# A four-layer block on one core: the order of y, z and the clamp on VectorE and ScalarE, and the place of one product on TensorE

## The reference, cut to what matters

```
proj = h @ in_proj_w.T                        # gate, x, B, C and dt
hBC  = silu(conv4(x, B, C))                   # causal, 4 taps, one filter per channel
dt   = softplus(dt + dt_bias);  A_dt = -exp(A_log) * dt;  x_dt = x * dt
# chunks of 128 tokens, two in a sequence; 128 heads of 64, in 8 groups that share B and C
Y_diag = (C·B * exp(segment_sum(A_dt))) @ x_dt            # within a chunk
Y_off  = C @ (state left by the chunk before) * decay     # across, second chunk of a sequence only
y = Y_diag + Y_off + D * x
y = rmsnorm(y) * norm_w * silu(gate)
out = y @ out_proj_w.T
```

## Time and profile before

| | us |
|---|---|
| median of 3 runs | 1646.56 |
| the profiled execution | 1649.56 |
| its span, first to last instruction | 1647.8 |
| PE busy in the span | 1592.1 (97%) |
| PE weight loads busy | 1305.5 (79%) |
| DVE busy | 1358.0 (82%) |
| ACT busy | 1281.6 (78%) |
| POOL busy | 801.7 (49%) |

### The profile page before, as it was taken

The page is one execution under the profiler, slowest core; times in us unless marked ns, Lnnn a source line. Parts: engine busy times, 40 slices in busy tenths (PEclk is TensorE's granted clock), DMA queues, the critical chain, the costliest instruction groups (busy, mean ns, idle before and its releaser), DMA issues.

```text
span 1647.8 us, 27075 instructions
## 1 busy us (share of the span) xinstructions
PE 1592.1 (97%) x8984; PEld 1305.5 (79%) x8984; DVE 1358.0 (82%) x2199; ACT 1281.6 (78%) x2218; POOL 801.7 (49%) x806
## 2 busy tenths in 40 slices
PE   6999999999999999999999999999999999999988
PEld 5888777788888887888788788888788888888766
DVE  5887886888888888887888887898888888878766
ACT  4454459888989798979987898888888888798842
POOL 3565124554556455545554454544554555454460
PEclk9999999999999999999999999999999999999999
DMA  5320345455565446545555455545554645445321
GB/s 174 120 91 1 111 133 155 143 161 148 140 179 153 146 130 176 155 129 150 170 143 160 135 170 143 173 115 172 152 160 131 166 145 160 144 142 161 116 71 52
DMA packets 186074, 229.56 MB, mean 139 GB/s; under 512 B 22384, under 2 KB 122096, under 8 KB 184272
## 3 DMA queue, kind: packets, MB, share of 16 engines
q1 hardware_dynamic: 185936, 227.84, 46.6%
HBM read 190.02 MB, written 37.75 MB: 138 GB/s over the span
## 4 chain that ended last, share of the span: by engine, by line
PE 43%; DVE 20%; issue 9%; ACT 7%; DMA 7%; SPq 1%; POOL 1%; DVEq 0%; ACTq 0%; POOLq 0%
PE bank L160 8%; PE bank L162 7%; PE bank L161 7%; DVE m_xc L1955 7%; PE bank L2343 4%; PE bank L2347 4%; PE bank L2309 4%; PE bank L2344 4%; DMA m_x_rows<-x_turned_rows 4%; DMA x_turned_rows<-m_x_blocks 3%; DVE m_gate L1955 3%; ACT m_mt L1661 2%; DVE m_y L2047 2%; PE bank L2331 2%; DVE xdt L2000 1%
## 5 line engine op out<-in xcount | busy, mean ns | idle before, releaser
L160 PE MATMUL bank<-xh,w_h 128*128 128x512 f32 x1152 | 463.4, 402 | 6.9 <-DVE m_xc L1955 3.9
L162 PE MATMUL bank<-xh,w_l 128*128 128x512 f32 x1152 | 450.9, 391 | 0.0
L161 PE MATMUL bank<-xl,w_h 128*128 128x512 f32 x1152 | 450.5, 391 | 0.0
L1569 POOL TENSOR_TENSOR m_z_l<-m_zg,m_z_h 128x512 fp32r<-128x512 f32 x128 | 179.4, 1401 | 458.2 <-ACT m_z_h L1715 458.2
L1551 POOL TENSOR_TENSOR w_l<-w_raw,w_h 128x512 fp32r<-128x512 f32 x142 | 203.6, 1434 | 228.2 <-ACT w_h L1629 228.2
L1661 ACT ACTIVATE m_mt<-m_mt,m_unit 128x128 f32<-128x128 f32 x1024 | 312.3, 390 | 0.0
L160 PEld LDWEIGHTS bank<-xh,w_h 128*128 128x128 f32 x1152 | 217.1, 188 | 61.9 <-issue 18.9
L162 PEld LDWEIGHTS bank<-xh,w_l 128*128 128x128 f32 x1152 | 216.9, 188 | 46.1
L1955 DVE SCALAR_TENSOR_TENSOR m_xc<-bank,m_par_slots,m_xc 128x1020 f32<-128x1020 f32 (+2 forms) x192 | 243.9, 1270 | 9.9 <-ACT m_xc L1640 5.4
L161 PEld LDWEIGHTS bank<-xl,w_h 128*128 128x128 f32 x1152 | 217.4, 189 | 40.4
L2343 PE MATMUL bank<-m_wo_h,m_z_h 128*128 128x512 f32 x512 | 205.0, 400 | 9.2 <-ACT m_z_h L1715 8.6
(11 more groups left out here) (315 smaller groups left out, 2857.2 us busy)
## 6 DMA issues: line engine op xcount, KB each, us to landing
m_mt<-ncs_rows SPq DMA_DIRECT2D x128, 512.0 KB, 5.8
w_raw<-w_in SPq DMA_DIRECT2D x144, 256.0 KB, 4.2
x_turned_rows<-m_x_blocks SPq DMA_DIRECT2D x120, 256.0 KB, 3.9
m_x_rows<-x_turned_rows SPq DMA_DIRECT2D x480, 64.0 KB, 2.3
m_wo_raw<-w_out_in SPq DMA_DIRECT2D x64, 256.0 KB, 3.9
m_e<-ecs_rows SPq DMA_DIRECT2D x128, 128.0 KB, 3.7
a_wo_raw<-wo_in SPq DMA_DIRECT2D x8, 1024.0 KB, 5.0
x<-x_in SPq DMA_DIRECT2D x8, 256.0 KB, 4.3
```

The source lines that it names most:

```text
L160: nc.tensor.matmul(out, ah, bh, start=first, stop=False)
L161: nc.tensor.matmul(out, ah, bl, start=False, stop=False)
L162: return nc.tensor.matmul(out, al, bh, start=False, stop=last)
L1569: nc.gpsimd.tensor_tensor(z_l[:, s % 2, :, :], zg[:], f(z_h[:, s % 2, :, :]), ALU.subtract).then_inc(zl_ready, 1)
```

## The change

Four edits go together. Nothing is added or taken away; every engine runs the same operations on the same tiles, in another order.

1. VectorE, paired steps: y and z of chunk s-1 are made ahead of `add_out(s-2)` and, in even steps, ahead of `times_dt(s)`. In odd steps they stay behind the first block transpose.
2. ScalarE: `decay` is cut into `clamp` (the eight Relu) and `decay` (the exponential). Outside steps 1 and 9 the order is clamp, z's high part, square, exponential; it was clamp, exponential, square, high part. In steps 1 and 9 only high part and square change places.
3. TensorE: `across` stands right behind the pair's masked products in every odd step; it stood between the two halves of the step's tile.
4. GpSimd: where the last group's second half begins and in it, `to_chunk_end` of chunk s+1 is made at the end of odd step s, not at the end of step s+1.

```
@@ gpsimd, step @@
-                if s % 2 == 0 and own(kind):
+                if s % 2 == 0 and own(kind) and paired(kind, s):
                     to_chunk_end(g, s)
+                if s % 2 == 1 and turned_by_tensor(kind, s):
+                    to_chunk_end(g, s + 1)
@@ scalar @@
-            def decay(g, s):
+            def clamp(g, s):
...
                 last.then_inc(clamped, 1)
+
+            def decay(g, s):
+                g, s = g + s // STEPS, s % STEPS
                 act.wait_ge(clamped, at(g, s))
...
             def square_and_high(g, s):
+                act.wait_ge(z_ready, at(g, s))
+                act.wait_ge(out_done, at(g, s - 2))
+                nc.scalar.activation(z_h[:, s % 2, :, :], zg[:], ACT.Copy).then_inc(zh_ready, 1)
                 act.wait_ge(y_ready, at(g, s))
                 act.wait_ge(sq_summed, at(g, s - 1))
                 nc.scalar.activation(ysq[:], y[:], ACT.Square).then_inc(sq_ready, 1)
-                act.wait_ge(z_ready, at(g, s))
-                act.wait_ge(out_done, at(g, s - 2))
-                nc.scalar.activation(z_h[:, s % 2, :, :], zg[:], ACT.Copy).then_inc(zh_ready, 1)
@@ scalar, step @@
-                if ahead(kind, s + 2) and not (kind == "lead" and s == STEPS - 1):
+                clamps = ahead(kind, s + 2) and not (kind == "lead" and s == STEPS - 1)
+                if clamps:
+                    clamp(g, s + 2)
+                if clamps and not (paired(kind, s) and t != 1):
                     decay(g, s + 2)
...
                 if paired(kind, s) and t != 1:
                     for made in made_in(kind, s):
                         square_and_high(g, made)
+                    if clamps:
+                        decay(g, s + 2)
@@ vector, step @@
+                for made in turned_in(kind, s)[:1]:
+                    turn_blocks(g, made)
+                if paired(kind, s):
+                    for made in made_in(kind, s):
+                        make_y(g, made)
+                        make_z(g, made)
+                if behind(kind, s - 2):
+                    add_out(g, s - 2)
                 for made in scaled_first(kind, s):
                     times_dt(g, made)
-                for made in turned_in(kind, s)[:1]:
-                    turn_blocks(g, made)
-                if behind(kind, s - 2):
-                    add_out(g, s - 2)
...
-                if paired(kind, s):
-                    for made in made_in(kind, s):
-                        make_y(g, made)
-                        make_z(g, made)
@@ tensor, step @@
-                if own(kind) and s % 2 == 1 and not paired(kind, s):
+                if own(kind) and s % 2 == 1:
                     across(g, s, kind)
...
-                    if own(kind) and s % 2 == 1 and paired(kind, s):
-                        across(g, s, kind)
```

## The result

The changed kernel takes 1672.20 us (median of 4 runs, 1669.52 to 1674.92), the kernel before 1644.51 (4 runs, 1642.15 to 1646.75): a ratio of 1.0170, with a 95% interval of 1.0151 to 1.0189. It is 27.7 us slower. I had forecast 1620.5, range 1611 to 1637, with a chance of 0.07 for slower. The profiled execution takes 1672.60 us (span 1670.9, granted clock 0.989), that of before 1649.56 (span 1647.8, clock 0.995).

A forecast was written before the change was run, and what follows sets the result against it. TensorE was taken as the bound, busy 1284.0 of 1300 us in the paired steps. Terms 9.9 + 3.5 - 1 + 4 + 9.5 = 25.9 us off the profiled 1649.56; as a median 1620.5, range 1611 to 1637.

The forecast's parts named there:

- Part 1: Paired steps, y and z first on VectorE, high part ahead of the exponential: 9.9 and 3.5 us of TensorE waits go.
- I charge 1 us for the eight steps 4 together: Even steps without taps: VectorE idles while the next x rows are read; cost 1 us, bounds 0 to 8.
- Part 2: TensorE, across beside the masked products in paired steps: 4 us won, bounds -2 to 8.4.
- slack of 0.7 us: Even step without taps: time left between the second xdt and the masked products that need it, 0.7 us.
- The handover itself: VectorE, even step without taps: 3.63 us from the end of one xdt to the start of the next.
- Three taps cover the transfer: Even steps with taps: three taps on VectorE cover the transfer of the next x rows; nothing charged.
- My term of 0.10: TensorE, paired steps: one fewer start behind plain fp32 products per pair, each costing about 0.10 us more.
- no new wait is charged: Across needs m_xdd 2.86 us sooner, but the z chain comes earlier: no wait charged, bound 4 us.
- Part 3: Last half of the last group, m_xdd a step earlier on GpSimd: 9.5 us won, bounds 6 to 10.
- The unnamed wait: TensorE ahead of across in the last half: 9.0 us in 4 places, taken to be m_xdd.
- D: Rival, slower: in even steps without taps masked products wait for the second xdt; 1656 us at 1.6 us stall; chance 0.09.

The follow-up runs named there:

- x_first: The changed kernel with xdt of the even chunk first on VectorE again, y and z still ahead of add_out: 1623.21 us, ratio 0.9852.
- x_first_bare: The changed kernel with xdt first in the steps without taps (0, 4, 8), late in those with taps: 1660.20 us, ratio 1.0092.
- across_only: The kernel before with edit 3 alone, across right behind the pair's masked products: 1650.27 us, ratio 1.0030.
- without_vector: The changed kernel with VectorE's old order, so edits 2, 3 and 4 without 1: 1633.28 us, ratio 0.9912.
- pool_only: The kernel before with edit 4 alone, GpSimd's m_xdd a step earlier in the last half: 1634.39 us, ratio 0.9922.
- w_low_late: The changed kernel with GpSimd's low part of the weights behind z's low part and the squares in even paired steps: 1663.26 us, ratio 1.0103.

## Why the prediction was wrong

**The step that failed** is in Part 1: "I charge 1 us for the eight steps 4 together; bounds 0 to 8." These eight steps cost 32.1 us in the trace of after (some 21 of stall, 11 of slow clock), and the place of `xdt` in all even steps, for most of which I had charged nothing, 53 us. With `xdt` left first, as in x_first, the change gives 25.5 us, where my sum without this term was 26.9. That they lie so close is in part luck: x_first has in it 7 us for the last across, which I had not charged, and 3 us less from part 2 than forecast, and yet its paired steps are 16.1 us shorter (1526.41 against 1542.51) where I had 17.4, so gains that I had not listed made up for both. The term failed in three ways.

*The slack of 0.7 us was worked out with durations of another company.* I put y, z, `add_out` and `xdt` at 3.9 us, from 814.00 to 817.9, by durations of operations with nothing beside them. In group 2 of after they take 655.84 - 649.95 = 5.89: the second addition 1.64 in place of 0.69, `xdt` 1.85 in place of 0.76. GpSimd's two operations, each released by ScalarE, stand beside them. I had also 8.0 us from the start of y to the masked products, and it is 657.16 - 649.95 = 7.2. So 2.0 + 0.8 us went against a slack of 0.7: 2.1 us, where 2.6 are measured. The second `xdt` brings it to 2.5: it takes 1.30 in place of 0.76, beside GpSimd's operation at 658.72, and the handover ahead of it 0.16 less. The handover itself was right at this place: 3.63 us in the earlier trace rows, 655.84 to 659.31 = 3.47 in after, 3.4 to 3.8 in the eight groups.

*"Three taps cover the transfer" asked only for VectorE's wait.* In steps with taps `xdt` stands ahead of the taps, and whatever makes it longer or VectorE later moves the taps, which free the bank for TensorE's tile. The late `xdt` also moves `m_xdd` and the rows of the next chunks. All three are in the 40 us of these steps (x_first_bare); their shares were not separated.

*The clock was left out.* Six of the eight stalls cost more behind them: 1.6 us in five groups (12.6 us for the pair against 11.04) and 2.9 in group 7 (13.98).

**Part 1, the gains,** came as worked out: in the paired steps the waits for z's high part and for y ahead of C·B are gone in after and in x_first (but for 0.15 us there). But they belong to edits 1 and 2 together; edit 2 alone gave 1.6 us, y and z earlier without it nothing.

**Part 2** was mis-sized: 4 us forecast, 0.02 for each pair measured, 1 us in all, which is inside the bounds of -2 to 8.4. My term of 0.10 for one fewer start behind plain fp32 products did not come, since across beside the masked products takes 858.13 - 857.21 = 0.92 where it took 0.81. The rule of the Trainium skill that I had weighed against it (TensorEngine Tiling (Array Packing), Key Properties) gave 0 for this term, and the trace agrees with it better than with my 4. And "no new wait is charged" missed one: I had asked for m_xdd only, not for the bank that across writes. In the last paired step that bank is read by VectorE's `xdt`, some 7 us in after, 5 in across_only. Nor was m_xdd always in time: in without_vector, with the old order on VectorE, across waits 5.1 us in 11 places, each time until 0.10 us after `m_xdd`, a little above my bound of 4; in x_first it does so once, 0.3 us.

**Part 3** was right: 10.2 us in the account of the trace, 11.1 in pool_only, 9.5 forecast, bounds 6 to 10. The unnamed wait was m_xdd: all four starts of across in before lie 0.10 us after its end.

**The rivals.** D was the mechanism, with a chance of 0.09 and a price of 1656. It named the second `xdt`, the open handover and the steps without taps; of these only steps 4 stall in all eight groups, while steps 0 do in one and steps 8 in none. Of its formula, each microsecond beyond 3.63 + 0.7, the form was right and the length that grew was the wrong one: not the transfer but the operations ahead of it. It left out the steps with taps. The rule that I set beside D (the Trainium skill, SBUF — State Buffer, SBUF: two separate sides: VectorE with two SBUF inputs and GpSimd lock a shared port, and the loser blocks) agrees with the trace, 0.69 against 1.64 and 0.76 against 1.85 us; I had written that by it the slack would go, and did not put that into the chances. D's condition, 1.2 us of stall per step, was within reach of rows that I had: with single `xdt` operations at their longest, 1571 ns in place of 426, the slack of 0.7 is gone.

## What to carry to other kernels

Before an operation is moved behind others, ask what its end releases: here it is a read from memory into the single buffer that the next one needs, and the distance from one to the next was never under 3.4 us, and other work used to cover it. Take the slack with the durations that the operations have beside the other engine's work in the new order, and if it is smaller than one such lengthening, treat it as gone. When a product is moved, check every buffer that it writes as well as those it reads, in the first and last rounds too, where a tile has another role.

## What the runs showed of the hardware

- VectorE's operations with two inputs, neither of them a bank, take up to 3 times as long beside GpSimd's: y's second addition 0.69 and 1.64 us, two `xdt` operations 0.76 and 1.85 (2.35 in w_low_late), the mask 1.21 and 2.29. Those that read a bank did not lengthen in the paired steps of before, after and w_low_late: y's four operations at most 0.35 us each, `add_out` 0.69, `scale_across` 0.69, one of the taps 1.28.
- The handover of `m_x_rows` from the end of one `xdt` over four reads of 64 KB to the start of the next takes 3.47 us in after and 653.11 - 649.71 = 3.40 in w_low_late, 3.63 in the earlier trace rows. Where VectorE idles through the whole of it in after it is 3.4 to 3.6 us in most places and up to 5.2 in some (85.0 us in 23 waits).
- Behind an idle time of TensorE of 2.45 us (the eight steps 5 of after) the granted clock over the next 3.3 us was 0.50 to 0.63 in six places and 1.00 in two (groups 0 and 5), and behind 4.65 us it was 0.65 for 7.2. Behind 1.40 us (x_first_bare, 713.82) it stayed 1.00, and the products were 0.23 us apart again from the second on.
